# One visits product per tree, one bank per kernel-v block, and late weights split by GpSimd alone

## The reference

```
h = patchify(x) @ tok_W.T + tok_b                       # 64 x 196 x 256
xn = rms_norm(layernorm(h)); uv = silu(xn @ uv_w.T)     # u: 512, v: 512, base: 128
q, k = rope(base * gamma + beta)
kernel = square(relu((q @ k.T + w_rel[j - i]) / sqrt(128)))
h = h + layernorm(h) * res_scale + (u * (kernel @ v)) @ o_w.T
logits = layernorm(h) @ W_in.T + b_in                   # 8 trees x 255 nodes
# each tree: walk from the root, right if the node's logit > 0, 7 levels;
# keep silu(logit) of the 8 nodes on the walk, zero elsewhere
out = h + (silu(logits) * visited) @ W_out.T
```

## Time and profile before

| | |
|---|---|
| median of three runs | 2283.66 us |
| span of the profiled execution, first to last instruction | 2279.8 us |
| mean granted clock of PE | 0.991 |
| busy: PE, PEld | 2216.3 us (97%), 2080.7 us (91%) |
| busy: DVE, ACT, POOL | 1800.4 us (79%), 1154.4 us (51%), 252.6 us (11%) |
| PE in the two stretches 0 to 60 and 60 to 120 us | 33.95 and 47.42 us busy, clock 0.83 and 0.86 |
| PE in the loop, 260 to 330 us | 69.38 of 70 us busy, clock 1.00 |

### The profile page before, as it was taken

One profiled execution on the slowest core, in us unless ns is written; L12 is line 12 of the kernel. 1 busy time (PEld: TensorE's weight loads), 2 busy tenths in 40 slices (PEclk: granted clock), 3 DMA queues, 4 the chain that ended last, 5 costly groups with the idle time before them and its releaser, 6 DMA issues.

```text
span 2279.8 us, 37943 instructions
## 1 busy us (share of the span) xinstructions
PE 2216.3 (97%) x12992; PEld 2080.7 (91%) x12992; DVE 1800.4 (79%) x3539; ACT 1154.4 (51%) x2248; POOL 252.6 (11%) x221
## 2 busy tenths in 40 slices
PE   5799999999999999999999999999999999999998
PEld 4799999999999999999999999999999999999998
DVE  6688887788887788877888877888778888778885
ACT  3355554555554555544555545555545555445453
POOL 4101111001111001110011110011100011100110
PEclk8899999999999999999999999999999999999999
DMA  3100000000000000000000000000000000000000
GB/s 126 56 29 7 21 28 28 28 28 0 28 28 28 28 17 11 28 28 28 28 2 26 28 28 28 24 4 28 28 28 28 12 16 28 28 28 28 0 18 15
DMA packets 36667, 58.79 MB, mean 26 GB/s; under 512 B 4174, under 2 KB 29744, under 8 KB 36656
## 3 DMA queue, kind: packets, MB, share of 16 engines
q1 hardware_dynamic: 36656, 58.65, 8.6%
HBM read 45.79 MB, written 12.85 MB: 26 GB/s over the span
## 4 chain that ended last, share of the span: by engine, by line
PE 85%; DVE 8%; issue 3%; ACT 2%; DMA 1%; POOL 0%; SPq 0%; DVEq 0%; ACTq 0%; POOLq 0%
PE front L899 8%; PE front L901 8%; PE front L900 8%; PE hid_ps L899 8%; PE out_acc L899 8%; PE hid_ps L900 8%; PE hid_ps L901 8%; PE out_acc L901 8%; PE out_acc L900 8%; PE hid_ps L1071 4%; PE front L934 3%; PE front L927 2%; DVE tok_major L658 2%; PE front L1030 2%; DVE tok_major L237 2%
## 5 line engine op out<-in xcount | busy, mean ns | idle before, releaser
L462 ACT ACTIVATE hid<-hid_ps,col 128x392 f32<-128x392 f32 x512 | 284.9, 583 | 281.4 <-PE hid_ps L901 227.8
L899 PE MATMUL hid_ps<-ffn_x,in_lo 128*128 128x392 f32 x1024 | 366.9, 358 | 1.2 <-DVE ffn_x L564 1.2
L899 PE MATMUL out_acc<-hid_hi,outw_lo 128*128 128x392 f32 x1024 | 365.9, 357 | 0.0
L900 PE MATMUL hid_ps<-ffn_x,in_hi 128*128 128x392 f32 x1024 | 351.2, 343 | 0.0
L901 PE MATMUL hid_ps<-ffn_x,in_hi 128*128 128x392 f32 x1024 | 350.2, 342 | 0.0
L901 PE MATMUL out_acc<-hid_hi,outw_hi 128*128 128x392 f32 x1024 | 349.0, 341 | 0.0
L900 PE MATMUL out_acc<-hid_lo,outw_hi 128*128 128x392 f32 x1024 | 348.9, 341 | 0.0
L748 DVE SCALAR_TENSOR_TENSOR hid<-hid_ps,hid 128x784 f32<-128x784 f32 x256 | 248.4, 970 | 64.2 <-PE hid_ps L1071 64.2
L307 POOL TENSOR_TENSOR inv_root<-to_root,minus_half 98x8 f32<-98x8 f32 x64 | 106.7, 1668 | 1629.8 <-DVE to_root L604 920.1
L338 ACT ACTIVATE hid_hi<-hid 128x784 fp32r<-128x784 f32 x256 | 218.7, 854 | 132.7 <-PE out_acc L901 116.9
L564 DVE TENSOR_TENSOR hid_lo<-hid,hid_hi 128x784 fp32r<-128x784 f32 x256 | 247.3, 966 | 22.4 <-ACT hid_hi L338 22.4
(11 more groups left out here) (121 smaller groups left out, 4790.3 us busy)
## 6 DMA issues: line engine op xcount, KB each, us to landing
x_raw<-x SPq DMA_DIRECT2D x192, 196.0 KB, 2.4
out<-out_stage SPq DMA_DIRECT2D x32, 392.0 KB, 2.4
hid<-in_w SPq DMA_DIRECT2D x8, 256.0 KB, 3.1
hid<-out_w SPq DMA_DIRECT2D x8, 256.0 KB, 3.4
tok_major<-tok_w SPq DMA_DIRECT2D x3, 256.0 KB, 4.2
u<-uv_w SPq DMA_DIRECT2D x1, 576.0 KB, 5.1
hid<-o_w SPq DMA_DIRECT2D x2, 256.0 KB, 6.0
h_kept<-uv_w SPq DMA_DIRECT2D x1, 288.0 KB, 5.4
```

The lines of the kernel that those rows point to most:

```text
L462: act.activation(hid_t[:, t % 2, b], hid_ps[:, t % 2, b, 0:T], ACT.Silu, bias=c(COL_B_IN + 2 * t + b)).then_inc(activated, 1)
L899: pe.matmul(out, w[1], x_parts[0], start=start, stop=False)
L900: pe.matmul(out, w[0], x_parts[1], start=False, stop=False)
```

## The change

1. **Visits.** The 128 leaves are put in another order, so that the leaf in row r lies below the inner node in row r. One table `toward` (128x128) holds 15 times the inner node's table plus the leaf's. One matmul into the leaf bank gives both answers: at least -0.5 means the leaf is visited, at least -15.5 the inner node. `tree_visits` is one matmul instead of two, and waits for the decisions and for the leaf silu only. `mask` becomes two DVE instructions of 392 columns with the two thresholds; the second waits for the inner silu as well. `tree_logits(t, 0)` no longer waits for the mask of tree t - 2 but for its silus; `tree_logits(t, 1)` waits for the mask.
2. **Leaf order on the chip.** The host's arrays stay as they were. For out_w and the leaf bias the order is made by DMAs (8 strided runs of rows beside the main part, so 9 DMAs for each out_w piece); for in_w POOL splits in 9 strided pieces, 9 CAST and 9 subtractions instead of one each.
3. **Kernel-v.** `mix(n, e)` makes 12 matmuls of 196 columns that add hi and lo in one bank of both images. `copy_mix` and `sum_mix` are gone, and `gate` reads the bank.
4. **Late weights.** Own staging tensor of four slots; POOL splits all 18, DVE none. SP's order changes: constants for the first steps are 2 DMAs, tables come behind uv_w, and x loads of unit 1 and 2 stand between late pieces. The first round of the loop is written out (`body(0, 1)`), and in it PE waits for each piece where it is used.

The core of the diff:

```diff
@@ late weights
+        late_raw = sb("late_raw", [P, LATE_RING, LATE], F32)        # LATE_RING 3 -> 4
+        def late_parts(n, part):
+            dst, src = late[n][part], late_piece(n)
+            if LATE_PARTS[n] == 1:
+                return [(dst, src)]
+            return [(dst[:, :, 0:P], src[:, :, 0:P])] + [
+                (dst[:, :, P + row:P + row + rows], src[:, :, P + leaf:P + leaf + step * (rows - 1) + 1:step])
+                for row, leaf, step, rows in LEAF_RUNS]
@@ SP
+            def load_late(ns):
+                for n in ns:
+                    if n >= LATE_RING:
+                        sp.wait_ge(late_lo, late_done(n - LATE_RING))
+                    landed = late_in[n % LATE_RING]
+                    src, dst = late[n][0], late_piece(n)
+                    if LATE_LOADS[n] == 1:
+                        sp.dma_start(dst, src).then_inc(landed, 16)
+                        continue
+                    sp.dma_start(dst[:, 0], src[:, 0]).then_inc(landed, 16)
+                    for row, leaf, step, rows in LEAF_RUNS:
+                        sp.dma_start(dst[row:row + rows, 1],
+                                     src[leaf:leaf + step * (rows - 1) + 1:step, 1]).then_inc(landed, 16)
...
+            load_late(range(O_PIECES, LATE_RING))
             load_x(1, range(XRING))
+            load_late(range(LATE_RING, LATE_EARLY))                  # pieces 4 to 7
+            load_x(1, range(XRING, XC))
+            load_late(range(LATE_EARLY, PIECES))                     # pieces 8 to 17
+            load_x(2, range(XRING))
@@ POOL
-            split_late((0,))
             norm_roots(0, 0)
-            split_late(range(1, 5))
+            split_late(range(0, 2))
             rotate_k(0)
-            split_late(range(5, len(POOL_PIECES)))
+            split_late(range(2, 5))
             norm_roots(0, 1)
+            split_late(range(5, 10))
+            norm_roots(1, 0)
+            split_late(range(10, 13))
+            rotate_k(1)
+            split_late(range(13, PIECES))
+            norm_roots(1, 1)
@@ DVE
             def gate(n, e):
-                dve.wait_ge(summed, PAIR * (EC * n + e + 1))
-                dve.scalar_tensor_tensor(u_t[:, e], mix_sum[e % 2][:, :], 1.0 / S, u_t[:, e],
+                dve.wait_ge(mixed, EC * n + e + 1)
+                dve.scalar_tensor_tensor(u_t[:, e], front[:, BANK_MIX[e], 0:T], 1.0 / S, u_t[:, e],
                                          ALU.mult, ALU.mult).then_inc(gated, 1)
             def mask(i, t):
                 dve.wait_ge(visits_ready, TREES * i + t + 1)
-                dve.scalar_tensor_tensor(hid_t[:, t % 2], hid_ps[:, t % 2, :, 0:T], 0.0, hid_t[:, t % 2],
-                                         ALU.is_ge, ALU.mult).then_inc(masked, 1)
+                for b in (1, 0):
+                    if b == 0:
+                        dve.wait_ge(activated, 2 * (TREES * i + t + 1))
+                    dve.scalar_tensor_tensor(hid_t[:, t % 2, b], hid_ps[:, t % 2, 1, 0:T], VISITED[b],
+                                             hid_t[:, t % 2, b], ALU.is_ge, ALU.mult).then_inc(masked, 1)
@@ PE
+                for m in range(PAIR):
+                    for j in range(2):
+                        parts = [kern_parts[:, m, j, p] for p in range(2)]
+                        last = product(front[:, BANK_MIX[e], m * L:(m + 1) * L],
+                                       [v[:, 2 * m + j, at] for v in (v_hi, v_lo)], parts,
+                                       j == 0, j == 1)
+                last.then_inc(mixed, 1)
...
             def tree_visits(i, t):
-                pe.wait_ge(activated, 2 * (TREES * i + t + 1))
-                for b in range(2):
-                    last = pe.matmul(hid_ps[:, t % 2, b, 0:T], toward[:, b], decide[:, t % 2],
-                                     start=True, stop=True)
+                pe.wait_ge(decided, TREES * i + t + 1)
+                pe.wait_ge(activated, 2 * (TREES * i + t) + 1)
+                pe.matmul(hid_ps[:, t % 2, 1, 0:T], toward[:, :], decide[:, t % 2],
+                          start=True, stop=True).then_inc(visits_ready, 1)
...
             body(None, 0)
-            pe.wait_ge(pool_late_lo, len(POOL_PIECES))
-            pe.wait_ge(dve_late_lo, len(DVE_PIECES))
-            with pe.Fori(0, UNITS - 1) as i:
+            body(0, 1)
+            with pe.Fori(1, UNITS - 1) as i:
```

More of the change, by code:

```diff
@@ L53 @@
 UV = 2 * E + S
-LATE, LATE_RING = 512, 3
-PIECES = 2 + 2 * TREES
-DVE_PIECES = (1, 3, 5, 7, 9, 17)
-POOL_PIECES = tuple(n for n in range(PIECES) if n not in DVE_PIECES)
-LATE_ORDER = (0, 1, 2, 4, 3, 6, 8, 5, *POOL_PIECES[5:7], 7, *POOL_PIECES[7:9], 9, *POOL_PIECES[9:], 17)
-CONST_DMAS = 5
+LATE, LATE_RING = 512, 4
+O_PIECES = 2
+PIECES = O_PIECES + 2 * TREES
+LEAF_RUNS = tuple((2 ** d - 1, 2 ** (DEPTH - 1 - d) - 1, 2 ** (DEPTH - d), 2 ** d)
+                  for d in range(DEPTH)) + ((INNER, INNER, 1, 1),)
+LATE_PARTS = tuple(1 + len(LEAF_RUNS) if n >= O_PIECES and n % 2 == 0 else 1 for n in range(PIECES))
+LATE_LOADS = tuple(1 + len(LEAF_RUNS) if n >= O_PIECES and n % 2 == 1 else 1 for n in range(PIECES))
+CONST_DMAS = 2
+LATE_EARLY = 8
+TABLE_DMAS = 3 + len(LEAF_RUNS)
 MOMENT_STEPS = (11, 7)
@@ L157, in vit_tower @@
         toward_raw = u[:, UV:UV + 2 * P].rearrange("p (b n) -> p b n", b=2)
-        late_raw = [hid[:, n * LATE:(n + 1) * LATE] for n in range(LATE_RING)]
         late = [(o_w[:, n * 2:n * 2 + 2], o_hi[:, n * 2:n * 2 + 2], o_lo[:, n * 2:n * 2 + 2])
-                for n in range(2)]
+                for n in range(O_PIECES)]
         for t in range(TREES):
@@ L271, in _ @@
                 sp.dma_start(dst, src).then_inc(uv_w_in[n], 16)
-            for n in LATE_ORDER:
-                if n in DVE_PIECES[1:]:
-                    sp.wait_ge(dve_late_lo, DVE_PIECES.index(n))
-                elif n in POOL_PIECES[2:]:
-                    sp.wait_ge(pool_late_lo, POOL_PIECES.index(n) - 1)
-                sp.dma_start(late_raw[late_slot(n)],
-                             late[n][0].rearrange("p a b -> p (a b)")).then_inc(late_in[late_slot(n)], 16)
-            load_x(1, range(XRING))
-            with sp.Fori(0, UNITS - 2) as i:
+            for dst, src in ((rope_t[:, :, :], rope), (toward_raw, anc), (rel_bias[:, :, :], rel)):
+                sp.dma_start(dst, src).then_inc(tables_in, 16)
+            load_late(range(O_PIECES))
+            for row, leaf, step, rows in LEAF_RUNS:
+                src = cols[leaf:leaf + step * (rows - 1) + 1:step, COL_B_IN:COL_B_IN + 2 * TREES]
+                sp.dma_start(leaf_col[row:row + rows], src).then_inc(tables_in, 16)
+            load_late(range(O_PIECES, LATE_RING))
+            load_x(1, range(XRING))
+            load_late(range(LATE_RING, LATE_EARLY))
+            load_x(1, range(XRING, XC))
+            load_late(range(LATE_EARLY, PIECES))
+            load_x(2, range(XRING))
+            store(0)
+            with sp.Fori(1, UNITS - 2) as i:
                 load_x(i + 1, range(XRING, XC))
@@ L314, in rotate_k @@
             def rotate_k(n):
+                if first(n):
+                    pool.wait_ge(tables_in, TABLE_DMAS * 16)
                 rotate(pool, n, 1, k_step)
@@ L654, in scale_base @@
                     return
+                if first(n) and which == 1:
+                    dve.wait_ge(const_in, CONST_DMAS * 16)
                 dve.tensor_scalar(rot[2 * which], base[:, :], c(COL_GAMMA + which), c(COL_BETA + which),
@@ L764, in final, with build_toward @@
                                   ALU.add).then_inc(out_ready, 1)
-            def to_bf16():
-                dve.wait_ge(const_in, CONST_DMAS * 16)
-                dve.tensor_copy(toward[:, :, :], toward_raw).then_inc(toward_ok, 1)
+            def build_toward():
+                dve.wait_ge(tables_in, TABLE_DMAS * 16)
+                for row, leaf, step, rows in LEAF_RUNS:
+                    at = slice(leaf, leaf + step * (rows - 1) + 1, step)
+                    dve.scalar_tensor_tensor(toward[:, row:row + rows], toward_raw[:, 0, row:row + rows],
+                                             ABOVE - 1.0, toward_raw[:, 1, at],
+                                             ALU.mult, ALU.add).then_inc(toward_ok, 1)
             def uv_low(ns):
@@ L825, in body @@
                 rotate_q(n)
-                if first(n):
-                    split_late(2)
                 v_low(n, 0)
@@ L889, in _ @@
             body(None, 0)
-            with dve.Fori(0, UNITS - 1) as i:
+            body(0, 1)
+            with dve.Fori(1, UNITS - 1) as i:
                 body(i, i + 1)
@@ L1055, in tree_logits @@
                     pe.wait_ge(ffn_x_lo_ok, 2 * (i + 1))
+                if first(i) and b == 0:
+                    pe.wait_ge(late_lo, late_done(O_PIECES + 2 * t))
                 if t >= 2 and b == 0:
-                    pe.wait_ge(masked, TREES * i + t - 1)
+                    pe.wait_ge(activated, 2 * (TREES * i + t - 1))
+                elif t >= 2:
```

(3 more changed lines are left out.)

141 lines of the change are left out of this document (44 added, 97 removed).

## The result

The changed kernel takes 2263.96 us (median of four runs, 2262.11 to 2265.53); in the same rounds the kernel before takes 2283.64 us. The ratio is 0.9916, 95% interval 0.9902 to 0.9930: faster by 0.84%. The forecast was 2260 us, with a range of 2243 to 2274. The profiled execution has a span of 2260.3 us against 2279.8, 19.5 less, where 23.9 had been forecast. The profiled execution is the fastest of the four (2262.11 us).

The account below looks back on a forecast made before the run. PE's matmul stream was taken to bound the loop. Units -14.9 (-0.48 times 31), last trees -4, unit 0 -9 and unit 1 +4 take the span from 2279.8 to 2255.9; 3.9 to the median gives 2260 us, range 2243 to 2274.

Parts of the forecast that it names:

- Visits, -1.36 per unit: PE's stream in the loop: eight visits matmuls of 0.17 us go per unit, with nothing covering them.
- Kernel-v, +0.56 per unit: PE's stream: twelve narrow matmuls paced by weight loads take 1.30 us a block against 1.16, four blocks per unit.
- narrow matmuls run at their own 0.09: Rival for kernel-v: a block takes 1.08 us instead of 1.30, 27 us less, 2233 us; chance 0.10.
- Masks, +0.21 each: DVE: two mask instructions of 392 columns take 1.10 us where one of 784 took 0.89.
- the +0.13 there: Chain from swap_base to v_full: tree 3's mask pushes it by 0.21 us less 0.1 of room, +0.13 per unit.
- the +0.19: Output of tree 6: PE waits for hid_low, so one visits matmul's saving is gone, +0.19 us per unit.
- more is given back to DVE: Rival in the loop: further DVE chains cost 0.3 us per unit in all, +9 us, 2269 us; chance 0.20.
- Unit 0, -9: Start: late splits leave DVE, kernel-v's path shortens by 5.4 us, tables come later; -9 us (-4 to -12).
- Unit 1, +4: Peeled round: POOL's late weight pieces hold PE by 3 us and SP adds to it; +4 us (0 to +12).
- Last trees, -4: End: tree 1's visits skip the 2.4 us inner silu wait, eight matmuls save 1.4; -4 us (0 to -5).
- the slower one: Rival: POOL's splits become the start, holding 30 us at 11.8 us per in_w piece; 2286 us, chance 0.04.
- the longer hold: Rival in unit 1: POOL needs 6.7 us per in_w piece and the hold is about 12 us; 2268 us, chance 0.09.

Follow-up runs that it names:

- experiment 3: The changed kernel with its single visits matmul issued twice, one behind the other: 2301.76 us, ratio 1.0081.
- experiment 1: The changed kernel with the old kernel-v product put back, copy_mix and sum_mix included: 2242.73 us, ratio 0.9822.
- Experiment 2: The changed kernel with kernel-v matmuls loading 96 of 128 weight columns, 32 features of each block left out: 2231.97 us, ratio 0.9774.
- experiment 4: The changed kernel with one wide matmul placed after every second narrow kernel-v matmul, same matmuls in all: 2266.04 us, ratio 0.9921.
- Experiments 5 and 7: 5: changed kernel with late pieces 8 and 9 issued, 10 and 11 split sooner, 2258.36 us; 7: that plus the old kernel-v product, 2238.82 us.
- experiment 6: The changed kernel with in_w split in two POOL instructions per piece, its leaf reordering left out: 2257.13 us, ratio 0.9888.

## Why the prediction was right, and where its terms were off

The forecast of 2260 us missed 2264 by 4 us, inside its own range. The mechanisms were the ones named; several terms had another size, and some of their misses cancel, which is luck. One place that gave back stood among the rivals and not in the sum, and the lower clock behind a wait stood in no term.

- **Visits, -1.36 per unit: right.** 0.167 x 8 = 1.34, in the phases and again in experiment 3.
- **Kernel-v, +0.56 per unit: the mechanism right, the term 0.19 too small.** It is +0.75 by phase 5-6 and 0.74 by experiment 1. The form "11 load distances of 0.11 plus 0.09" is what the rows show; it comes to 1.32 instead of 1.30, and the wide matmul behind the block is held up too, for another 0.03: together 0.05 for each of four blocks. The old trace had the held-up wide one already, inside the 1.16. Experiment 2 shows that the load decides. The prediction's sentence that 0.09 is seen only in the scores is a wrong reading: the kernel-v rows before have it once in each call (1030.24 to 1030.33), behind a wide matmul. The rival "narrow matmuls run at their own 0.09" fell by the rows, and weaving (experiment 4) didn't make it true.
- **Masks, +0.21 each: too much by three times.** Two halves are 0.95 against 0.89. The row taken for one half (0.55) is an instruction of another form, with a column as scalar operand. A nearer row stood in the same trace: `gate` before is the same operation with constants at 392 columns, from SBUF, and holds DVE for 0.48 (1031.60 to 1032.08), which would have given +0.07. So the chain to `swap_base` did not grow: the 0.06 fit into the 0.1 of room, the wait for v_full stayed at 0.62, and the +0.13 there was nothing. At the output of tree 6 the +0.19 was 0.03.
- **The give-back outside the sum: 0.11 per unit** at the transposes of hT, behind ACT's copy. The rival "more is given back to DVE" named the chain after the visits of tree 1, but with DVE as the engine, and priced such places at 0.3 in all on top of the sum. Of that came 0.11, and the engine was ACT; with the 0.03 at tree 6 all give-back is 0.14, less than the 0.32 that the sum itself had for its two places.
- **The unit: -0.48 forecast, -0.43 measured.** The misses nearly cancel: +0.02 for visits, +0.19 for kernel-v, -0.29 for the two chains that didn't grow as far, +0.11 for the place outside the sum, 0.03 in all against the 0.05 that the rounds show.
- **Unit 0, -9: measured -9.4, with terms off both ways.** Kernel-v began 6.22 us sooner (49.00 against 55.22) where 3.6 were forecast, and from there to the projection 8.35 us passed, where 6.0 were forecast and 11.44 had been. The matmuls themselves ran without a wait, but from about 51.4 us on at the lower clock, where narrow ones start 0.21 apart (52.66 to 52.87): 28 of the 48, which costs an estimated 28 x 0.10 = 2.8 us. The two misses cancel, and experiment 3's start, with the clock at its upper level there, was 3.5 us shorter. That -9 was hit within 0.4 is luck.
- **Unit 1, +4: measured +8.0** (+7.6 against a round that is otherwise 0.43 shorter), the largest miss. POOL's price for a piece was right (4.3 against 4.2 at its quickest). The waits came to 4.1 us instead of 3: piece 12's instructions took 5.4 us, and piece 8 started late behind the x loads. The 2.7 us at the lower clock behind the long wait stood in no term. Of the 1.2 us left, 0.5 and 0.4 are waits for tok_major and kern (97.18 and 123.32), while the usual 0.62 for v_full is missing here; about 1 us stays unplaced. Experiments 5 and 7 show that the hold comes from where the pieces stand in the order of loads and splits.
- **Last trees, -4: measured -4.7.** The wait of 2.4 us became 0.6, so 1.8 of the 2.4 came; eight visits matmuls are 1.34. The remaining 1.5 us is the stretch at the lower clock that followed the wait before and is gone after (8 wide matmuls 0.33 instead of 0.18 apart are 1.2 of it); no term had it.
- **From span to median, 3.9: came out at 3.7.** An execution's time lies 1.8 to 2.0 us above its own span; the rest is that both profiled executions were about 2 us faster than the median of their kernel, which need not repeat.

In sum: (0.480 - 0.434) x 31 = 1.4 us for the units, 4.0 for unit 1, less 0.4 for unit 0 and 0.7 for the end: 4.3 us, against 4.4 between the forecast span of 2255.9 and 2260.3. Of the rivals, the slower one needed 11.4 us for an in_w piece and the longer hold 6.7; the rows have 4.2 to 5.4.

## What to carry to other kernels

Where PE's stream is the bound, count matmuls as well as columns: a matmul in a row of its like costs about the larger of its columns and its own weight load, here 0.11 us for 128 weight columns, and cutting wide ones into narrow ones costs that in every round even where it frees two other engines. Price a new form of instruction by a row of that form, with the same operands, and not by one of the same width. And where a warm-up round is held, look at the order of loads and splits first: moving two loads and two splits won 4.8 of 8 us, and in the profiled execution the hold of 4.1 us cost 2.7 more at the lower clock. Look up which unit a longest wait lies in before it is put down to one: in experiment 6 the 4.1 of PE's wait list lies in unit 0 and not in unit 1.
